# Expert feed-forward: the 176 middle rows divided 112 + 64 in place of 88 + 88, and the down weights loaded in two transfers

## The reference

```
scores = softmax(x @ gate_weight.T)                 # 64 experts, 8 groups, best 3 groups
topk_w, topk_i = top_k(scores of those groups, 6)   # 6 experts of a token
buf = 96 slots for each expert, filled with its tokens            # (64, 96, 256)
g = einsum('ech,emh->ecm', buf, Wg)                 # m = 176 middle rows
u = einsum('ech,emh->ecm', buf, Wu)
out = einsum('ecm,ehm->ech', silu(g) * u, Wd)       # back to 256 channels
y = sum over the 6 experts of out[slot] * topk_w
return y + shared expert (352 middle rows, all tokens)
```

## Time and profile before

| | |
|---|---|
| time, median of 3 runs | 1286.99 us (1285.45 to 1289.58) |
| the profiled execution's own time | 1283.71 us |
| its span | 1281.9 us |
| PE busy | 985.2 us, 77% |
| ACT, DVE, POOL busy | 728.9, 523.4, 423.7 us |
| mean granted PE clock | 0.88 |
| DMA | 94,927 packets, 176.11 MB |

### The profile page before, as it was taken

One profiled execution on the slowest core, in us unless ns is written; L12 is line 12 of the kernel. 1 busy time (PEld: TensorE's weight loads), 2 busy tenths in 40 slices (PEclk: granted clock), 3 DMA queues, 4 the chain that ended last, 5 costly groups with the idle time before them and its releaser, 6 DMA issues.

```text
span 1281.9 us, 18696 instructions
## 1 busy us (share of the span) xinstructions
PE 985.2 (77%) x6520; PEld 594.9 (46%) x6520; DVE 523.4 (41%) x1532; ACT 728.9 (57%) x960; POOL 423.7 (33%) x408
## 2 busy tenths in 40 slices
PE   4886868778887788787554999955587863999973
PEld 3633323322332323222334999943344442999962
DVE  7744431156221233230441333337776741333327
ACT  2285989999999999999101444414434400344420
POOL 3100000000222003234043565530098985556550
PEclk9878888998999998999686999976698976999985
DMA  9990000000111001100583999748133434899947
GB/s 352 394 393 31 1 1 1 1 17 1 42 47 37 17 16 60 39 20 6 148 254 92 292 295 289 177 118 273 50 116 117 123 109 106 243 293 284 261 72 305
DMA packets 94927, 176.11 MB, mean 137 GB/s; under 512 B 13119, under 2 KB 46880, under 8 KB 94833
## 3 DMA queue, kind: packets, MB, share of 16 engines
q1 hardware_dynamic: 58416, 130.55, 30.4%
q0 software_dynamic: 23616, 28.44, 10.4%
q10 hardware_dynamic: 12800, 15.93, 4.5%
HBM read 107.30 MB, written 83.72 MB: 149 GB/s over the span
## 4 chain that ended last, share of the span: by engine, by line
PE 32%; DVE 5%; DMA 3%; issue 3%; SPq 2%; POOL 2%; ACT 2%; DVEq 1%; POOLq 0%; ACTq 0%
PE PS L1323 13%; PE PS L1334 8%; PE PS L1261 4%; PE PS L1393 2%; PE PS L1310 2%; POOL expert_in L307 2%; SPq L1116 1%; DMA spare_space<-expert_out 1%; DMA normed<-xp 1%; SPq L1117 1%; PE PS L1246 1%; DMA XE<-expert_in 1%; PE PS L1270 1%; DMA expert_out<-ob,yidx 1%; POOL expert_out L1209 1%
## 5 line engine op out<-in xcount | busy, mean ns | idle before, releaser
L307 POOL DMA_INDIRECT expert_in<-xp,didx x192 | 192.9, 1005 | 621.7 <-ACT PR L684 483.9
L679 ACT ACTIVATE PR<-PS 128x1024 f32<-128x1024 f32 (+3 forms) x320 | 275.4, 935 | 55.7 <-PE PS L578 40.7
L684 ACT ACTIVATE PR<-PR 128x2048 f32<-128x2048 f32 (+3 forms) x160 | 272.4, 1705 | 0.0
L1209 POOL DMA_INDIRECT expert_out<-ob,yidx x128 | 180.6, 1411 | 148.2 <-ACT ob L1502 108.3
L587 PE MATMUL PS<-PR,V 128*32 128x512 f32 (+3 forms) x1280 | 164.8, 590 | 80.4 <-ACT PR L684 80.3
L575 PE MATMUL PS<-QT,KT 96*128 96x512 bf16 (+3 forms) x640 | 177.5, 372 | 19.8 <-ACT PR L679 16.9
L1740 DVE SCALAR_TENSOR_TENSOR gta<-gth,PS 88x192 f32<-88x192 f32 x128 | 44.8, 350 | 193.6 <-ACT gth L1492 193.6
L575 PEld LDWEIGHTS PS<-QT,KT 96*128 96x128 bf16 x640 | 59.3, 103 | 130.3 <-ACT PR L679 89.7
L1492 ACT ACTIVATE gth<-PS 88x192 f32<-88x192 f32 x128 | 41.7, 326 | 107.8 <-PE PS L1323 107.8
L1323 PEld LDWEIGHTS PS<-XT,spare_space 128*88 128x88 f32 x960 | 92.5, 164 | 8.8 <-issue 2.6
L1502 ACT ACTIVATE ob<-PS,wslot 96x256 f32<-96x256 f32 x128 | 60.1, 469 | 61.9 <-PE PS L1334 59.6
(11 more groups left out here) (257 smaller groups left out, 1355.3 us busy)
## 6 DMA issues: line engine op xcount, KB each, us to landing
spare_space<-in_wgu SPq DMA_DIRECT2D x60, 352.0 KB
expert_out<-zero SPq DMA_DIRECT2D x2, 8256.0 KB, 50.4
expert_in<-zero SPq DMA_DIRECT2D x2, 7776.0 KB, 39.3
XE<-expert_in ACTq DMA_DIRECT2D x32, 486.0 KB, 9.8
WGU<-in_wgu SPq DMA_DIRECT2D x44, 352.0 KB
spare_space<-expert_out SPq DMA_DIRECT2D x24, 512.0 KB, 6.1
spare_space<-in_wd SPq DMA_DIRECT2D x60, 176.0 KB
shared_space<-in_wgu SPq DMA_DIRECT2D x24, 352.0 KB
```

The costliest lines, as they stand in the source:

```text
L307: pool.indirect_dma_start(out=buf_d[f], out_offset=bass.IndirectOffsetOnAxis(ap=didx[b][:, r, j:j + 1], axis=0), in_=xp[b][:, r, :], in_of ...
L679: act.activation(PR[:, n % 3, 2 * pr:2 * pr + 2, cols(c, s):CW], PS[:, S0 + 2 * pr:S0 + 2 * pr + 2, cols(c, s):CW], ACT.Tanh, scale=1.0 / ...
L684: act.activation(PR[:, n % 3, :, lo:CW], PR[:, n % 3, :, lo:CW], ACT.Exp, scale=SOFT_CAP).then_inc(exp_done, 1)
L1209: pool.indirect_dma_start(out=y_d[f], out_offset=bass.IndirectOffsetOnAxis(ap=yidx[:, n % 4, j:j + 1], axis=0), in_=ob[:, i % EU, :], in_o ...
```

## The change

The 176 middle rows are divided into `MA` = 112 and `MB` = 64. The columns of `wgu` are laid in a new order: gate 0:112, up 0:112, then gate 112:176 and up 112:176 side by side, 128 columns. gate_up makes three pieces of them: 112 columns into PSUM columns 0:96, 112 columns into 192:288, and the 128 into 96:192, so that the last 64 gate rows stand on partitions 0:64 and the last 64 up rows on partitions 64:128 of the same columns. DVE's second step is divided in two, 112 x 96 and 64 x 96; the second reads up from partitions 64:128. down adds a product over 112 rows and one over 64. `wd` comes in two transfers of 112 and 64 rows of 1024 bytes, so a load adds 48 to the semaphore. ACT's tanh runs over 112 partitions. Sizes of tiles grow with it.

```diff
-MH = M // 2
+MA = 112
+MB = M - MA
...
-            return wgu, wd, ring_ld[x], 32 * loads
+            return wgu, wd, ring_ld[x], 48 * loads
...
                 sp.dma_start(wgu, wgu_d[e]).then_inc(loaded, 16)
-                sp.dma_start(wd, wd_d[e]).then_inc(loaded, 16)
+                sp.dma_start(wd[:, 0, :], wd_d[e, 0:MA, :]).then_inc(loaded, 16)
+                sp.dma_start(wd[0:MB, 1, :], wd_d[e, MA:M, :]).then_inc(loaded, 16)
...
-                    for j in range(4):
+                    for j, at, width in ((0, 0, MA), (2, MA, MA), (1, 2 * MA, 2 * MB)):
                         for hh in range(CH):
-                            last = pe.matmul(PS[0:MH, 4 + e % 2, j * CAP:(j + 1) * CAP], wgu[:, hh, MH * j:MH * (j + 1)],
+                            last = pe.matmul(PS[0:width, 4 + e % 2, j * CAP:(j + 1) * CAP], wgu[:, hh, at:at + width],
                                              XT[:, h % 2, e % EH, hh, :], start=(hh == 0), stop=(hh == CH - 1))
...
-                    for m in range(2):
-                        last = pe.matmul(PS[0:CAP, 6 + e % 2, 0:C], ha[:, e % 2, m, :], wd[:, m, :],
+                    for m, width in enumerate((MA, MB)):
+                        last = pe.matmul(PS[0:CAP, 6 + e % 2, 0:C], ha[0:width, e % 2, m, :], wd[0:width, m, :],
                                          start=(m == 0), stop=(m == 1))
...
-                    act.activation(gth[:, e % 2, :], PS[0:MH, 4 + e % 2, 0:2 * CAP], ACT.Tanh, scale=0.5).then_inc(gate_tanh, 1)
+                    act.activation(gth[:, e % 2, :], PS[0:MA, 4 + e % 2, 0:2 * CAP], ACT.Tanh, scale=0.5).then_inc(gate_tanh, 1)
...
-                    bank = PS[0:MH, 4 + e % 2, :]
-                    dve.scalar_tensor_tensor(gta[:], gth[:, e % 2, :], 1.0, bank[:, 0:2 * CAP], ALU.add, ALU.mult)
-                    dve.drain()
-                    dve.scalar_tensor_tensor(ha[:, e % 2, :, :].rearrange("p m s -> p (m s)"), bank[:, 2 * CAP:4 * CAP], 0.5,
-                                             gta[:], ALU.mult, ALU.mult).then_inc(act_ready, 1)
+                    bank = PS[:, 4 + e % 2, :]
+                    dve.scalar_tensor_tensor(gta[:], gth[:, e % 2, :], 1.0, bank[0:MA, 0:2 * CAP], ALU.add, ALU.mult)
+                    dve.drain()
+                    dve.scalar_tensor_tensor(ha[:, e % 2, 0, :], bank[0:MA, 2 * CAP:3 * CAP], 0.5, gta[:, 0:CAP], ALU.mult, ALU.mult)
+                    dve.scalar_tensor_tensor(ha[0:MB, e % 2, 1, :], bank[MB:2 * MB, CAP:2 * CAP], 0.5, gta[0:MB, CAP:2 * CAP],
+                                             ALU.mult, ALU.mult).then_inc(act_ready, 1)
                     dve.drain()
...
-        ("wgu", np.concatenate([Wg, Wu], 1).transpose(0, 2, 1).reshape(E, CH, P, 2 * M).transpose(0, 2, 1, 3)),
-        ("wd", Wd.transpose(0, 2, 1).reshape(E, 2, MH, C).transpose(0, 2, 1, 3)),
+        ("wgu", np.concatenate([Wg[:, 0:MA], Wu[:, 0:MA], Wg[:, MA:], Wu[:, MA:]], 1).transpose(0, 2, 1).reshape(E, CH, P, 2 * M).transpose(0, 2, 1, 3)),
+        ("wd", Wd.transpose(0, 2, 1)),
```

More of the change, by code:

```diff
@@ L1048, in hybrid_kernel @@
         WD_space = keep("WD_space", [P, EU * 2 * C])
-        WD = WD_space[0:MH, :].rearrange("p (e m c) -> p e m c", e=EU, m=2)
+        WD = WD_space[0:MA, :].rearrange("p (e m c) -> p e m c", e=EU, m=2)
         XE = keep("XE", [CAP, 2, EH, RW])
         XT = keep("XT", [P, 2, EH, CH, CAP])
-        gth = keep("gth", [MH, 2, 2 * CAP])
-        gta = keep("gta", [MH, 2 * CAP])
-        ha = keep("ha", [MH, 2, 2, CAP])
+        gth = keep("gth", [MA, 2, 2 * CAP])
+        gta = keep("gta", [MA, 2 * CAP])
+        ha = keep("ha", [MA, 2, 2, CAP])
         ob = keep("ob", [CAP, EU, C])
@@ L1071, in ring_place @@
             return (space[:, at:at + CH * 2 * M].rearrange("p (h m) -> p h m", h=CH),
-                    space[0:MH, at + CH * 2 * M:at + WF].rearrange("p (m c) -> p m c", m=2))
+                    space[0:MA, at + CH * 2 * M:at + WF].rearrange("p (m c) -> p m c", m=2))
         def expert_weights(f, e):
```

## The result

The changed kernel takes 1316.49 us in the median of 6 runs (1314.23 to 1325.36), the kernel before 1286.22 us (6 runs, 1281.8 to 1289.58). The ratio is 1.0246, with a 95% interval from 1.0214 to 1.0278. I had forecast 1273 us and a range of 1262 to 1285. The time went the other way, and all of it was lost on PE inside the expert loop, at a place that I had priced at nothing: the product of down over 64 rows. It is the last sign that the prediction names: the step out of that product's second record takes 0.31 us and not 0.22.

The account below looks back on a forecast made before the run. PE, busy throughout both expert stretches, was taken as the bound. 1283.71 - 13.7 - 0.4 + 0.3 = 1269.9 us for the profiled execution, 1273.2 us as median; range 1262 to 1285.

Parts of the forecast that it names:

- the last sign that the prediction names: In down, a step from the 64-row product longer than 0.22 us would be a cost put at nothing.
- Down: Down's 4 records on PE: only the rows summed over change, so 0, with +-5 ns a record, +-2.6 us.
- Gate and up: Expert loop on PE: 16 records become 12, weight loads set the pace; 0.107 us an expert saved, 13.7 us.
- the first rival: Gate and up's weight loads cost nothing, PE's pace stays 82.2 ns at 112 and 128 columns: 1245 us; chance 0.10.
- the last step: Step from an expert's last gate and up record to the next operation on PE: some 84 ns.
- The second rival: Gate and up's loads of 112 columns cost what 128 do, so nothing gained: 1286 us; chance 0.13.
- One sum in the prediction: Gate and up's saving by the skill's load formula, 93 ns at 112 columns and 107 at 128: an estimated 19 us.
- ACT, DVE: Between gate and up and down: tanh 0; DVE's split step +0.15 us, hidden except behind each layer's last expert, 0.3 us lost.
- POOL, SP and the transfers: Expert loop's sends, 128 added issues and smaller down-weight packets: all stay hidden, 0.
- The third rival: Down weights' packets cost by number, not size; PE waits for last experts' weights: 1301 us; chance 0.10.
- The upper bound that the terms gave: Whole program: 112-column loads in gate and up at 111.6 ns, with down's +-2.6 us: 1288 us.

## Why the prediction was wrong

**The step that failed is "Down".** I wrote that only the rows that are summed over change and that nothing is added, with +-5 ns a record. It is +0.35 us an expert, 45 us: two switches, into the 64-row product and out of it. Less the 13 us that gate and up saves, that is 32 us, beside 31.6 measured. No row stood behind the 5 ns, and I took the number of rows to be without influence altogether.

The trace of before shows such switches, far from the expert loop. In the recurrence, products over 128 rows are followed by eight records over 64 rows, and these by products over 128 rows:

```profile
918.78 1.45 PE L1393 MATMUL PS<-spare_space,wab 128*128 128x512 f32 x3
...
920.16 1.59 PEld L1354 LDWEIGHTS PS<-O,WovT 64*128 64x128 f32 x8 [0.76 <-issue]
920.17 1.99 PE L1354 MATMUL PS<-O,WovT 64*128 64x256 f32 x8
...
922.09 0.10 PEld L1281 LDWEIGHTS PS<-selb,tri 128*128 128x128 bf16 x1 [0.33 <-issue]
922.09 0.20 PE L1281 MATMUL PS<-selb,tri 128*128 128x64 bf16 x1
```

The first three start 0.43 us apart, so the last at 919.64, and the first 64-row record follows 0.52 us later, together with its load. The last 64-row record starts at 921.78, and the next product follows 0.31 us later instead of 0.22. In both places it is 0.09 us more, with no wait in the profile.

The same is there on the column side. In the attention part, four products with 128 weight columns are followed by products with 32, which the code places side by side.

```profile
480.01 1.03 PE L575 MATMUL PS<-QT,KT 96*128 96x512 bf16 x4
...
480.97 1.06 PE L587 MATMUL PS<-PR,V 128*32 128x512 f32 x8
```

The four records start 0.22 us apart (512 columns in bf16), so the last at 480.67, and the next product follows 0.31 us later instead of 0.22. The profile names ACT (PR, L684) as what ended the idle time of the weight loads here, but ACT's instruction had ended at 480.80, and at 121.38 us the same step takes the same 0.31 us with no wait in the profile. It is again 0.09 us. The rows were there.

The Trainium skill has the rule too: "TensorEngine Tiling (Array Packing)", section "Key Properties", says "Mode switching requires drain", and the section on tiling modes lists 64 rows and 64 columns as modes of their own. I did not ask whether a product that merely is small falls under it. The runs here agree that it does, and put a price on it: 0.16 us a switch.

**Gate and up was right in kind and nearly in size.** The weight loads set the pace and the saving is there, against the first rival. The matmul and load durations in the changed kernel are 262 and 178 ns for 112 columns:

```profile
L1325 PEld LDWEIGHTS PS<-XT,WGU x528: 172/178/192, 737.2 to 1280.2; 128*112 128x112 f32 x132, 128*128 128x128 f32 x44
```

178 ns is what the line of 0.875 ns a column gives. In the padded kernel (down's second product filled up to 112 rows) a piece of 12 records takes 1.22 us, so 0.10 us an expert is saved and not 0.107. The starts are 98 and 112 ns apart, as forecast, but I had put the last step at 84 ns, and it takes 112, the pace of a record with 128 columns. 128 x 0.10 = 12.8 us, beside 11.4 us measured (8.4 to 14.7 by its interval). The first layer is 6.3 us shorter from its first gate and up to the start of its last down (692.03 to 837.58), and the second 6.5 us, against 6.9 forecast. The second rival (112 columns as dear as 128) is out. One sum in the prediction is off: with loads of 93 and 107 ns the saving comes to 20 us and not 19. Nothing rests on it.

**ACT, DVE.** Two DVE steps of 258 ns against 252 forecast:

```profile
L1744 DVE SCALAR_TENSOR_TENSOR ha<-PS,gta x128: 257/258/259, 703.1 to 1281.4; 112x96 f32<-112x96 f32 x128
```

`ha` is complete at 750.41 and the first load of its down begins at 751.24, 0.83 us later; in the padded kernel, whose loop is shorter, it is 0.48 us (746.06 to 746.54). It is hidden, as said. Behind the last expert of a layer it does show. The last down of the first layer, in the padded kernel and in the kernel before:

```profile
837.58 1.10 PE L1337 MATMUL PS<-WD_space,ha 112*96 112x256 f32 x4 [0.55 <-issue]
844.00 1.10 PE L1334 MATMUL PS<-WD_space,ha 88*96 88x256 f32 x4 [0.36 <-DVE ha L1742]
```

That is some 0.2 us a layer, where the sum has 0.15.

**POOL, SP and the transfers.** Hidden, as said: the run with two transfers alone shows no difference, and the padded kernel, in which the loop is shorter than before, still runs PE without a wait for a transfer. The third rival, the only one that I had on the slow side, had the sign right and the cause wrong; that its 1301 us lay nearer to the measured time than the forecast was luck.

**What I left out.** All three rivals and all my bounds were about loads and transfers, the parts that grow. The part that shrinks, a product of fewer rows, got no rival, though the last sentence of the prediction names the step to watch. The upper bound that the terms gave (1288) could not hold a mechanism that none of them named.

## What to carry to other kernels

Before a matmul is cut into unequal parts, look at both sizes of each part against 64. A part of at most 64 contraction rows (the rows that are summed over), or of 64 weight columns, among larger ones cost 0.16 us at each of its two borders here. Filling the 64 rows with zeros up to 112 took the price away, and 65 rows had no price to begin with. And a PE that is busy in every window may still be stopping: hold the starts of its records and the gaps between its weight loads beside the count.

## What the runs showed of the hardware

- The border lies between 64 and 65 rows (ratio 1.0325 against 1.0009). 64 weight columns among 88 cost as much (1.0336); where their border lies was not measured. 32 rows are as dear as 64 (1.0291 against 1.0325), and the price is paid per switch, not per record (1.0318 with twice the records).
- The price has two halves. The first record behind a switch starts 0.09 us later than usual (0.31 us for 0.22 behind a record of 256 columns), together with its own load; and the record behind it is late by another 0.07 to 0.09 us (0.29 us for 0.22 inside down, 0.17 for 0.09 inside gate and up of the changed kernel). The pause of the weight loads is not the price: it is 0.36 us behind records of 256 columns, where 0.05 us is usual (742.17 + 0.68 = 742.85, the next load at 742.90, with 65 rows), and 0.12 us behind the records of turn with 96 moving columns (742.59 + 0.72 = 743.31, the next load at 743.43, with both products over 64 rows). What PE does in that time is not something that these runs can tell.
- With weight columns above the moving ones, the load sets the pace of 32-bit products: 12 records with 112 and 128 weight columns and 96 moving ones take 1.22 us, against 12 x 0.082 = 0.98 us by the moving side.
- Packets of 1024 bytes in the place of half as many of 2048 moved the end of the weight stream by nothing that the windows show. The mean time of a packet in queue q1 fell from 107 ns (2235 bytes) to 88 ns (0.305 x 16 x 1281.1 / 71088; 1836 bytes).
